# Spreading the routing weights of a mixture of experts over the partitions: by broadcast transfers from DRAM, or by a matmul against a selector

## The reference

```python
shared_out = _silu_and_mul(xf @ shared_w1.T) @ shared_w2.T          # hidden 352
probs = softmax(xf @ gate_w.T)                                      # 16 experts
routing_weights, selected = top_k(probs, 6)
combine = zeros((T, 16)).at[arange(T)[:, None], selected].add(routing_weights)
gate_up = einsum('th,eoh->teo', xf, w1)                             # hidden 176 per expert
act = _silu_and_mul(gate_up)
moe_out = einsum('te,tei,ehi->th', combine, act, w2)
return moe_out + shared_out
```

## Time and profile before

| | |
|---|---|
| three executions | 766.93, 768.65, 772.71 us; median 768.65 us |
| the profiled execution | 772.71 us, with a span of 770.9 us |
| PE | busy 688.9 us (89%), mean granted clock 0.931 |
| DVE, ACT, POOL | busy 422.6, 313.1 and 259.0 us (55%, 41%, 34%) |
| transfers | 37.32 MB in all, mean 48 GB/s |

### The profile page before, as it was taken

The page is one execution under the profiler, slowest core; times in us unless marked ns, Lnnn a source line. Parts: engine busy times, 40 slices in busy tenths (PEclk is TensorE's granted clock), DMA queues, the critical chain, the costliest instruction groups (busy, mean ns, idle before and its releaser), DMA issues.

```text
span 770.9 us, 13166 instructions
## 1 busy us (share of the span) xinstructions
PE 688.9 (89%) x5188; PEld 560.3 (73%) x5188; DVE 422.6 (55%) x896; ACT 313.1 (41%) x748; POOL 259.0 (34%) x334
## 2 busy tenths in 40 slices
PE   4799999998898799958599988998699999999997
PEld 3565867765787587947476866776588888888886
DVE  5755687632348676464565555554553545454445
ACT  3340734534333242414476766566243232222322
POOL 4313232521425722221735343333314333433400
PEclk9977899987998699979799999899899999999999
DMA  6322100100112200000100000000043343333111
GB/s 207 94 69 72 50 3 2 29 2 1 50 42 61 62 1 22 0 21 22 41 2 21 1 2 2 1 1 1 2 118 111 99 132 105 96 116 124 60 37 55
DMA packets 18637, 37.32 MB, mean 48 GB/s; under 512 B 2544, under 2 KB 4720, under 8 KB 18576
## 3 DMA queue, kind: packets, MB, share of 16 engines
q1 hardware_dynamic: 18576, 36.48, 15.4%
HBM read 35.19 MB, written 1.11 MB: 47 GB/s over the span
## 4 chain that ended last, share of the span: by engine, by line
PE 71%; DVE 14%; ACT 7%; issue 5%; POOL 3%; DMA 1%; DVEq 0%; SPq 0%; POOLq 0%; ACTq 0%
PE ps L612 46%; PE ps L755 3%; PE ps L937 3%; PE ps L731 3%; PE ps L925 3%; PE ps L915 2%; PE ps L634 2%; PE ps L690 2%; ACT AO L1214 2%; PE ps L638 2%; PE ps L620 1%; DVE NB L1281 1%; PE ps L629 1%; ACT HHh L1131 1%; PE ps L705 1%
## 5 line engine op out<-in xcount | busy, mean ns | idle before, releaser
L1807 POOL TENSOR_SCALAR PB<-PB,sml 128x256 f32<-128x256 f32 x128 | 59.2, 482 | 94.2 <-DVE sml L1623 94.2
L1131 ACT CAST VVh<-U 128x512 fp32r<-128x512 f32 x50 | 31.1, 621 | 118.3 <-DVE U L1469 104.8
L612 PE MATMUL ps<-ATh,wh 128*128 128x512 f32 x176 | 71.9, 409 | 3.0 <-issue 1.4
L1461 DVE TENSOR_TENSOR U<-U,ps 128x512 f32<-128x512 f32 x50 | 34.4, 688 | 67.2 <-PE ps L612 67.2
L612 PE MATMUL ps<-ATl,wh 128*128 128x512 f32 x176 | 70.7, 402 | 0.0
L612 PE MATMUL ps<-ATh,wl 128*128 128x512 f32 x176 | 70.4, 400 | 0.0
L1776 POOL TENSOR_SCALAR wh<-wr 128x768 fp32r<-128x768 f32 (+3 forms) x31 | 24.1, 779 | 129.3 <-PE ps L612 126.3
L1202 ACT ACTIVATE PB<-ps,sml 128x256 f32<-128x256 f32 x128 | 59.5, 492 | 7.8 <-DVE sml L1617 7.7
L1778 POOL TENSOR_TENSOR wl<-wr,wh 128x768 fp32r<-128x768 f32 (+3 forms) x31 | 56.6, 1825 | 2.6
L1473 DVE TENSOR_TENSOR VVl<-U,VVh 128x512 fp32r<-128x512 f32 x50 | 34.6, 693 | 36.9 <-ACT VVh L1131 36.9
L1214 ACT COPY AO<-ps 128x512 f32<-128x512 f32 x64 | 35.0, 589 | 48.0 <-PE ps L925 47.8
(11 more groups left out here) (290 smaller groups left out, 2043.4 us busy)
## 6 DMA issues: line engine op xcount, KB each, us to landing
wr<-in_w SPq DMA_DIRECT2D x32, 384.0 KB, 3.1
wr<-in_w SPq DMA_DIRECT2D x16, 321.0 KB, 2.9
CB<-weights_of_experts SPq DMA_DIRECT2D x16, 256.0 KB, 3.9
wr<-in_w SPq DMA_DIRECT2D x11, 256.0 KB, 2.6
CB<-weights_of_experts SPq DMA_DIRECT2D x8, 224.0 KB, 3.5
CB<-weights_of_experts SPq DMA_DIRECT2D x8, 192.0 KB, 3.3
CB<-weights_of_experts SPq DMA_DIRECT2D x8, 160.0 KB, 3.4
XO<-in_x SPq DMA_DIRECT2D x2, 512.0 KB, 4.7
```

The source lines that it names most:

```text
L612: t = x.matmul(o, a, b, start=first and i == 0 and c == 0, stop=last and i == n - 1 and c == 2, skip_group_check=skip)
L1131: x.copy((VV if run == "moe" else HH)[c][0][:, :], b[:, :]).then_inc(*mark("hi", "h", run, j, half))
L1461: x.tensor_tensor(b[:, :], a[:, :], bank("u", run, j, half)[:, :], ALU.mult).then_inc(*vacates("u", run, j, half))
L1807: t = x.tensor_scalar(p[:, c, :], p[:, c, :], m[:, 16 + c:17 + c], 1.0, ALU.mult, ALU.mult)
```

## The change

The broadcast from DRAM is removed, with the DRAM tensor, the six `CB` tiles and all their transfers: two stores and 72 loads. In its place each of the 44 steps gets one more matmul (line 796 of the changed kernel): a constant 0/1 selector `SELr`, 128 columns of it for the chunk, is the stationary operand, and `CTr`, the turned routing weights of the half, is the moving one. It fills a PSUM bank (`"c"` in the ring of banks 4 to 7) with the weight of each hidden unit's expert, and DVE's multiplication reads that bank where it read `CB`.

So that the weights keep their accuracy in one float32r matmul, `route` makes a high and a low part of them (three more DVE operations on 128 × 64 elements) and `CTr` has 32 rows, high parts over low parts, with the selector holding the ones twice. The transposes give 32 rows where they gave 16. The matmul contracts over all 128 partitions, the other 96 rows of both operands being zero. To prepare this, a new item `selector` on POOL clears `CTr` (128 × 1024) and `SELr` (128 × 2816) and copies the selector to float32r (32 × 2816), and SP loads it from DRAM once (360 KB), ahead of the load of chunk moe5.

```diff
+            if run == "moe" and j >= 3:
+                b = fills(ring["w"], "c", run, j, half)
+                e.wait_ge(*at("selr"))
+                e.wait_ge(*vacated("sp", half))
+                x.matmul(b[:, :], SELr[:, (j - 3) * 128:(j - 2) * 128], CTr[:, sl], start=True, stop=True).then_inc(
+                    *filled("c", run, j, half))
...
         def spread(half):
-            if half == 0:
-                for s in latent_end():
-                    e.wait_ge(*s)
+            e.wait_ge(*at("blank"))
             e.wait_ge(*have("sp", half))
-            x.copy(CTr[:, half_cols(half)], bank("sp", half)[0:16, :]).then_inc(*vacates("sp", half))
+            x.copy(CTr[0:32, half_cols(half)], bank("sp", half)[0:32, :]).then_inc(*vacates("sp", half))
...
                 if run == "moe" and j >= 3:
-                    k = gated.index((j, half))
-                    e.wait_ge(*at(f"spread{k % NSPREAD}", k))
+                    e.wait_ge(*have("c", run, j, half))
                     e.wait_ge(*vacated("u", run, j, half))
-                    x.tensor_tensor(b[:, :], b[:, :], CB[k % NSPREAD][:, :], ALU.mult).then_inc(*mark("gated", k))
-                    S.same(("hid", run, j, half), ("gated", k))
+                    x.tensor_tensor(b[:, :], b[:, :], bank("c", run, j, half)[:, :], ALU.mult).then_inc(
+                        *vacates("c", run, j, half))
+                    S.value["hid", run, j, half] = vacated("c", run, j, half)
...
+        def selector():
+            for s in latent_end():
+                e.wait_ge(*s)
+            x.memset(CTr[:, :].bitcast(F32), 0.0).then_inc(*mark("blank"))
+            e.wait_ge(*at("sel"))
+            x.memset(SELr[:, :].bitcast(F32), 0.0).then_inc(*mark("selz"))
+            e.wait_ge(*at("selz"))
+            x.tensor_scalar(SELr[0:32, :], SELf[:, :], 1.0, 0.0, ALU.mult, ALU.add).then_inc(*mark("selr"))
...
-            if name.startswith("moe"):
-                while sent[0] < len(gated) and gated[sent[0]][0] + 3 * gated[sent[0]][1] <= int(name[3:]) - 3:
-                    spread()
+            if name == "moe5":
+                for s in latent_end():
+                    e.wait_ge(*s)
+                x_.dma_start(SELf[:, :], sel).then_inc(*mark("sel", by=16))
             load(name)
-        while sent[0] < len(gated):
-            spread()
```

More of the change, by code:

```diff
@@ L366, in plan @@
     split(9)
+    item("selector")
     def moe_after(half):
@@ L485, in program @@
     VV = [(sb(f"VVh{i}", [128, 512], R32, ctx=m1), sb(f"VVl{i}", [128, 512], R32, ctx=m1)) for i in range(3)]
-    CTr = sb("CTr", [16, T], ctx=m1)
-    routes = nc.dram_tensor("weights_of_experts", (16, T), F32, kind="Internal").ap()
-    CB = [sb(f"CB{i}", [128, 512], ctx=m1) for i in range(NSPREAD)]
+    SELf = sb("SELf", [32, 22 * 128], ctx=m1)
+    SELr = sb("SELr", [128, 22 * 128], R32, ctx=m1)
+    CTr = sb("CTr", [128, T], R32, ctx=m1)
     parts += [(sb(f"yh{i}", [128, SLOT], R32, ctx=m1), sb(f"yl{i}", [128, SLOT], R32, ctx=m1)) for i in range(2)]
@@ L493, in program @@
     n_units = len(us)
-    gated = [tuple(o[2:]) for o in order if o[0] == "step" and o[1] == "moe" and o[2] >= 3]
     cb = small("cb")
@@ L972, in spread @@
             for c in range(4):
-                p = x.transpose(b[0:16, c * 128:(c + 1) * 128], cl[:, half * 4 + c, :], ident)
+                p = x.transpose(b[0:32, c * 128:(c + 1) * 128], cl[:, half * 4 + c, :], ident)
             p.then_inc(*filled("sp", half))
@@ L1677, in route @@
             e.wait_ge(*now("dv"))
-            x.scalar_tensor_tensor(out=cl[:, hs, :], in0=rp[:, hs, 0:16], scalar=0.0, in1=pr[:, hs, 0:16], op0=ALU.is_lt,
-                                   op1=ALU.mult).then_inc(*mark("rt", half))
+            x.scalar_tensor_tensor(out=cl[:, hs, 16:32], in0=rp[:, hs, 0:16], scalar=0.0, in1=pr[:, hs, 0:16],
+                                   op0=ALU.is_lt, op1=ALU.mult).then_inc(*mark("dv"))
+            e.wait_ge(*now("dv"))
+            x.tensor_copy(chr_[:, hs, :], cl[:, hs, 16:32]).then_inc(*mark("dv"))
+            e.wait_ge(*now("dv"))
+            x.tensor_copy(cl[:, hs, 0:16], chr_[:, hs, :].bitcast(F32)).then_inc(*mark("dv"))
+            e.wait_ge(*now("dv"))
+            x.tensor_tensor(cl[:, hs, 16:32], cl[:, hs, 16:32], chr_[:, hs, :].bitcast(F32), ALU.subtract).then_inc(
+                *mark("rt", half))
         def store(t):
@@ L1816, in gpsimd @@
                     "memturn": memturn, "ffnmean": ffnmean, "expert": expert, "latstd": latstd, "l1norm": l1norm,
-                    "endnorm": endnorm})
+                    "endnorm": endnorm, "selector": selector})
     def sync(x_):
@@ L1834, in load @@
                 *mark(f"raw{i % NRAW}", name, by=16))
[L1836 to L1844, removed]
-                x_.dma_start(routes[:, half_cols(half)], CTr[:, half_cols(half)]).then_inc(*mark("routed", half, by=16))
-            e.wait_ge(*at("routed", half))
-            if k >= NSPREAD:
-                e.wait_ge(*at("gated", k - NSPREAD))
-            first = (j - 3) * 128
-            for x0 in range(first // 176, (first + 127) // 176 + 1):
-                a, b = max(x0 * 176, first) - first, min(x0 * 176 + 176, first + 128) - first
-                src = routes[x0:x0 + 1, half_cols(half)].to_broadcast([b - a, 512])
-                x_.dma_start(CB[k % NSPREAD][a:b, :], src).then_inc(
-                    *mark(f"spread{k % NSPREAD}", k, by=16))
         x_.dma_start(XO[:, 0:4, :], xv[:, 0:4, :]).then_inc(*mark("xin0", by=16))
```

4 lines of the change are left out of this document (2 added, 2 removed).

## The result

The changed kernel takes 788.42 us (median of 4, 781.2 to 788.72) against 767.79 us of the kernel before on the same chip (4 executions): a ratio of 1.0248, 95% interval 1.0206 to 1.029. Run again on another chip it took 786.24 us against 768.67, a ratio of 1.023. So it is slower, as forecast, but by about twice the 10.8 us forecast, and outside the range of 776 to 784 us.

What follows compares the result with a forecast made beforehand. The mixture of experts was taken as bound by PE's stream of matmuls alone. Selector matmuls 10.0, `route` of half 0 0.7 and transposes 0.1 gave 10.8 us on the 768.65 us median: 779.5 us, range 776 to 784.

Steps and rivals of the forecast that it cites:

- The selector matmuls: Mixture of experts, PE: 44 added matmuls, each costing its 0.2333 us start distance, the last not counting: 10.0 us.
- C: Rival, 6%: a selector matmul costs its row's 0.40 us, since it opens and closes its own bank; up to 786.7 us.
- The removed transfers: Mixture of experts: no engine waits for the broadcast transfers, so removing them gains nothing: 0.
- D: Rival, 3%: not slower, since without broadcasts and DVE's second SBUF read each 512-column matmul wins 0.020 us; 768 us.
- The multiplication and the ring of banks: Mixture-of-experts steps: DVE reads weights from PSUM as fast as `CB`, and no bank is late with three taken: 0 each.
- `route` of half 0: In the attention: three added DVE operations delay a closed loop that doesn't win time back: +0.7 us, bounds 0 and 0.7.
- A: Rival, 16%: a later wait on a third engine in the attention wins back the 0.7 us; 778.7 us.
- `route` of half 1: In the mixture of experts: three DVE operations ahead of a step's multiplication, covered by 1.05 us of slack: 0, bound 0.1.
- The transposes: Eight PE transposes with 32 columns of weights instead of 16: +0.1 us, bound 0.8.
- `selector` on POOL and SP: Start of the mixture of experts: memsets, copy and load finish 7 us before PE needs the selector: 0.
- B: Rival, 8%: POOL's memset of `SELr` holds up DVE's first low part, so PE starts 2 us later; 781.6 us.
- the row at 15.39 us: Evidence cited against B: small DVE operations with two inputs took 0.18 us under a memset of 15.2 to 17.0.

Runs made afterwards that it cites:

- the third memset: Kernel before plus the selector's POOL instructions, with the copy replaced by another memset of 2816 columns; no selector load or matmuls: 775.62 us, ratio 1.0074.

## Why the prediction was wrong

- **The selector matmuls, 10.0 us: right,** in mechanism and size. Starts 0.23 us apart, 10.14 us left when all else is taken out, 9.9 us when they are doubled. C (0.40 us each) is refuted for 128 rows; for 32 rows it would have been too low.
- **The removed transfers, 0: right.** PE's distance is 0.23 us with a transfer share of 0.12 as with 0.31. D is refuted.
- **The multiplication and the ring of banks, 0: right.** 688 ns, and no wait at line 796.
- **`route` of half 0, 0.7 us: right in kind, 0.5 measured.** Nothing absorbs it. From the low part ahead of the three operations to the second one behind them are 9.19 to 9.22 us in the six profiles that have the operations and 8.65 to 8.67 in the five that don't, and from there to the attention's last sum 25.81 to 25.86 in all eleven. So A is refuted.
- **`route` of half 1, "0, bound 0.1": wrong, 0.9 us.** I counted 0.7 us of delay against 1.05 us of slack. But the delay moved the low part from 0.17 us ahead of a POOL subtraction to 0.29 us behind its start, and it took 2.10 us instead of 0.69. What decides there isn't the delay but on which side of the split it falls.
- **The transposes, 0.1 us: nothing measured.** A load takes 99 ns instead of 88, and PE's starts don't move.
- **"`selector` on POOL and SP … 0": this is the step that failed,** with 4.3 us of wait and 0.9 of clock behind it. I looked at these instructions as work that someone waits for, and gave them 7 us of slack, which they had: PE never waited for the selector. Their cost lies in what they hold up on DVE while they run. That view I took only in B, and there only for the two low parts. The normalization ahead of them, whose 1.97 us and end beside POOL's subtraction I quote from the earlier trace rows as proof that the two engines hinder each other, I left out of the question: I placed the first low part at its old time and asked only what would lie over it. And the row at 15.39 us, an operation with two inputs, was the wrong witness for an operation with one. What the runs show in its place: three of POOL's instructions in a row hold the last normalization for 5.23 us instead of 1.97, the copy holds the first low part, and PE's first wait becomes 10.29 us instead of 5.99. With the same three instructions held back until later the wait is 5.98 us, and with them in the kernel before it is 10.29 us. About memsets against low parts B was argued rightly, as the third memset shows; the copy, which reads SBUF, was set aside because the second low part has slack, but since the normalization had pushed everything later, it caught the first.
- The range left out this case because B's price stopped at 2 us, the rest of one memset. The price of a hold-up is not always what is left of one instruction: here one DVE operation sat through a subtraction and two memsets. Of the measured 20.6 us the terms above explain 16.6; 768.65 + 16.6 = 785.3 us is outside the range already, so the miss doesn't hang on the 3.7 us of the medians that stay open.

## What to carry to other kernels

Work that is put on GpSimd "because it is idle" has two prices: whether someone waits for it, and which VectorE operations it holds while it runs. For the second, list what VectorE does under it, operation by operation, ahead of the critical one too, and sort by inputs; a pair of rows that is slowed already in the kernel before names the operation at risk, and as the upper bound of the new price take all of GpSimd's instructions that follow each other there. And zero rows in a small matmul's operands may be cheaper than a small matmul: here 0.23 us against 0.62.

## What the runs showed of the hardware that I had not expected

- A VectorE normalization of 128 × 256 elements, 1.38 us for four, was held for 5.23 us by three GpSimd instructions in a row (a subtraction and two memsets), although none of these is longer than 2.44 us. In these profiles a waiting normalization got in ahead of each GpSimd instruction that reads SBUF (the splits and the copy), in two places without a pause in the rows, and ahead of the third memset, which waited for GpSimd's own semaphore; it did not get in ahead of the other two memsets. Why not isn't shown.
- A matmul of 32 rows between matmuls of 128 rows costs 0.62 us where one of 128 rows costs 0.23.
- The length of PE's wait doesn't say how long the lower clock lasts behind it. After 10.28 and 10.29 us it lasted for the twelve down matmuls and then for two starts of 512 columns in one profile of the changed kernel and for five in the other; after 5.99 and 9.27 us for the same twelve and one; after 1.81 us it came 1.1 us later and lasted for the last down matmuls and four starts.
